# Order of the second FFN in a one-core macaron block: up products issued one block ahead of down products

## The chip, the core and the metric

The kernel runs on one core of one Trainium2 chip. The metric is the device time of one execution, in microseconds. The kernel before was timed three times: median 276.64 us, from 276.61 to 277.13. Its profiled execution took 276.34 us, of which 274.4 us are the span from the first to the last instruction in the trace.

## What is computed

The input is a residual `x` of 2048 tokens by 128 features, in float32. Three sublayers follow one another, the same FFN weights being used twice:

```
x = x + 0.5 * ffn(layernorm(x))     # first FFN
x = x + attention(layernorm(x))     # 16 heads of 8, strided and local keys
x = x + 0.5 * ffn(layernorm(x))     # second FFN
ffn(h) = butterfly_down(gelu(butterfly_up(h @ W_exp + b_exp) + up_bias)) @ W_con + b_con + down_bias
```

The hidden width of the FFN is 512. The butterflies are linear, so the kernel folds them into the two weight matrices at its start: `UPW` (128 by 512) and `DNW` (512 by 128, held as four 128 by 128 pieces). What is left of an FFN per block of tokens is an up product, a gelu and a down product.

## The kernel before

The 2048 tokens are cut into four blocks of 512 (`NB` = 4, `QB` = 512), each of four tiles of 128 (`TB` = 4). Blocks are numbered through: 0 to 3 are the blocks of the first FFN, 4 to 7 those of the second. Block 7 belongs to the tokens of the last attention block, 4 to those of the first. Every engine has its own instruction list, written out by hand, and engines meet only at semaphores; nothing is reordered by a planner.

One block of the second FFN takes these steps. VectorE normalizes its four tiles into `XN[b % 2]` (`normalize`, called by `ffn_ahead(b - 1)`, which first waits until the transposes of block b - 1 have been done). TensorE transposes them into PSUM bank 0 (`transpose_block`). ScalarE copies them into `XT` (`operand`), which waits until the up product of the block before has read `XT`. TensorE makes the up product (`ffn_up`), four chunks of 128 hidden units into banks 1 to 4, each written as two matmul instructions in the trace. ScalarE applies gelu, chunk by chunk (`gelu`), from those banks into the single buffer `GH`; before its first chunk it waits for the down product of the block before (`y_ps`). TensorE makes the down product (`ffn_down`): 4 tiles by 4 chunks, 32 matmul instructions in the trace, into bank 5 (the first two tiles of blocks 3 and 7 go to bank 0, `down_bank`); before it starts it waits for all four gelus (`g_ready`) and for VectorE's sum of the block before (`y_done`), which has to have read bank 5. VectorE adds the bias to the residual `X` (`add_bias`) and then the product (`ffn_sum`, in two halves for blocks 3 and 7). SyncE writes the finished block out.

In the last part of TensorE's list (lines 720 to 729) the order is: last value products of attention, transposes of block 4, `turn`, up product 4, `ctx_turn`, `project` (output projection of the last attention block, which waits for VectorE's copy `CTT`, line 1148); then for each block: its up product (block 4's is already there), the transposes of the next block, its down product. ScalarE's list there is gelu 4, operand 5, gelu 5, operand 6 and so on. VectorE's is: the last `finish_unit`, `finish_block(3)` (lines 1146 to 1151), the layernorm statistics of the last tokens, sum 4, then `ffn_ahead(5)` (which normalizes block 6), sum 5, `ffn_ahead(6)`, sum 6, sum 7. Block 5 has been normalized long before, within attention.

`ARENA` is a large SBUF tile; its first 8192 columns hold the attention probabilities (`PE_`).

Of the kernel before, what the change touches and what calls it, by code (L numbers as in the profile page):

```python
# [12 lines left out]
ACT = mybir.ActivationFunctionType  # L13
# [3 lines left out]
P = 128  # L17
S = 2048
NT = S // P
QB = 512  # L20
NB = S // QB
TB = QB // P
HID = 512
NC = HID // P
# [36 lines left out]
def program(nc, x, q_w, k_w, v_w, o_w, o_b, unity, w_exp_t, b_exp, up_near, up_far, up_b, dn_w, w_con, b_con, dn_b,  # L61
# [5 lines left out]
    with ctx:  # L67
        def sb(name, shape, dt=F32):
            return ctx.enter_context(nc.sbuf_tensor(name, shape, dt))

        def sem(name):
            return ctx.enter_context(nc.semaphore(name))
# [10 lines left out]
        GH = sb("gelu_h", [P, NC, QB])  # L83
# [6 lines left out]
        DNW = sb("down_folded", [P, NC, P])  # L90
        WCON = sb("w_con_sb", [P, NC, P])
        ARENA = sb("probs_all", [P, 10 * SC])
        BEX = sb("b_exp_sb", [P, NC])
        UBC = sb("up_bias_sb", [P, NC])
        BUP = sb("bias_up", [P, NC])
# [57 lines left out]
        PS = ctx.enter_context(nc.psum_tensor("ps", [P, 8, 512], F32))  # L153
# [35 lines left out]
        g_ready = sem("g_ready")  # L189
        y_ps = sem("y_ps")  # L190
        y_half = sem("y_half")
        y_first = sem("y_first")
        y_done = sem("y_done")
# [66 lines left out]
        def split_seen(b, part):  # L260
            return 4 * b + 4 if b < NB - 2 else 4 * (NB - 2) + 4 * last_splits.index((b, part)) + 4

        def down_bank(b, t):
            return PS[:, 0, :] if b % NB == NB - 1 and t < 2 else PS[:, 5, :]

# [161 lines left out]
        def _(pe):  # L427
# [9 lines left out]
            def ffn_up(b, chunks=range(NC)):  # L437

                pe.wait_ge(xt_ready, b + 1)
                if 2 <= b < NB:  # L440
                    pe.wait_ge(qk_ready, 3 * (b - 1))
                for c in chunks:
                    if 2 <= b < NB and c == 2:
                        pe.wait_ge(v_ready, 3 * (b - 1))
                    if b % NB:
                        pe.wait_ge(g_ready, NC * (b - 1) + c + 1)
                    pe.matmul(PS[:, 1 + c, :], UPW[:, c * P:(c + 1) * P], XT[:, :], start=True, stop=True).then_inc(h_ps, 1)  # L447
# [3 lines left out]
            for r in range(NC):  # L451
                mm = pe.matmul(PS[:, (6, 7, 4, 5)[r], :], ONE[32 * r:32 * r + 1, :], WUF[32 * r:32 * r + 1, :], start=True, stop=True)
# [5 lines left out]
            for j in range(NC):  # L458
                pe.wait_ge(wc_mix, j + 1)
                for o in range(NC):  # L460
                    mm = pe.matmul(PS[:, 2, j * P:(j + 1) * P], DNB[-1][:, j * P:(j + 1) * P], WCM[:, o, j, :],  # L461
                                   start=(o == 0), stop=(o == NC - 1))
# [4 lines left out]
            for j in range(NC):  # L467
                mm = pe.matmul(PS[:, 3, j:j + 1], UPB[STAGES - 3][:, j * P:(j + 1) * P], BEX[:, j:j + 1], start=True, stop=True)
            mm.then_inc(bup_ps, 1)
            pe.wait_ge(ld_wt, 16)  # L470
            for c in range(NC):
                pe.wait_ge(up_fold, STAGES - 2 + c + 1)
                mm = pe.matmul(PS[:, 1, :], WT[:, c, :], UPB[-1][:, c * HID:(c + 1) * HID], start=(c == 0), stop=(c == NC - 1))  # L473
# [6 lines left out]
            def ffn_down(b):  # L480
                if b == 0:
                    pe.wait_ge(dnw_sb, 1)
                pe.wait_ge(g_ready, NC * (b + 1))
                if b % NB:
                    pe.wait_ge(y_done, b)
                for t in range(TB):
                    for c in range(NC):
                        mm = pe.matmul(down_bank(b, t)[:, t * P:(t + 1) * P], GH[:, c, t * P:(t + 1) * P], DNW[:, c, :],  # L488
                                       start=(c == 0), stop=(c == NC - 1))
                    if t == 1 and b % NB == NB - 1:  # L490
                        mm.then_inc(y_half, 1)
                mm.then_inc(y_ps, 1)
# [92 lines left out]
            with nc.body("pe_large_bound", valid_engines=[pe.engine]):  # L585
                for b in range(NB):
                    pe.wait_ge(ld_ks[b], 16 * PARTS)
                for it in range(NB):
                    pe.wait_ge(ld_mq, 16 * (PARTS + 1) * NG * (it + 1))
                    for t in range(TB):  # L590
                        for j in range(NG + 1):
# [6 lines left out]
                            if j < NG:  # L598
                                for h in range(G):
                                    mm = pe.matmul(PS[:, half + h, :], QS[0:PROD, j, h, t * P:(t + 1) * P],  # L600
                                                   KS[0:PROD, :, G * j + h, :], start=True, stop=True)
                            else:
                                for c in range(2):
# [3 lines left out]
                                    for h in range(8):  # L607
                                        hh = 8 * c + h
                                        for w in range(2):
                                            q0 = t * P + w * W  # L610
                                            k0 = (2 * t + w) * WSTEP
                                            mm = pe.matmul(PS[w * W:(w + 1) * W, half + c, h * WIN:(h + 1) * WIN],
                                                           QS[0:PROD, hh // G, hh % G, q0:q0 + W],
                                                           KL[0:PROD, hh // G, hh % G, k0:k0 + WIN],
                                                           start=False, stop=(h == 7), skip_group_check=True)
# [67 lines left out]
            def ctx_turn(it):  # L683
                pe.wait_ge(o_ctx, 2 * NG * (it + 1))
                for t in range(TB):
                    mm = pe.transpose(PS[:, 7, t * P:(t + 1) * P], CT[:, t, :], ID[:, :])
                mm.then_inc(ct_ps, 1)

            def project(it):
                pe.wait_ge(ct_sb, it + 1)  # L690
                for t in range(TB):
                    mm = pe.matmul(PS[:, 7, t * P:(t + 1) * P], CTT[:, t * P:(t + 1) * P], OW[:, :], start=True, stop=True)  # L692
                mm.then_inc(op_ps, 1)
# [26 lines left out]
            turn(NB - 1, NG - 1)  # L720
            ffn_up(NB)
            ctx_turn(NB - 1)
            project(NB - 1)

            for b in range(NB, 2 * NB):
                if b > NB:
                    ffn_up(b)
                if b < 2 * NB - 1:
                    transpose_block(b + 1)
                ffn_down(b)  # L730

        @block.scalar
        def _(act):
# [15 lines left out]
            def gelu(b):  # L750
                for c in range(NC):
                    act.wait_ge(h_ps, NC * b + c + 1)
                    if b and c == 0:
                        act.wait_ge(y_ps, b)
                    if b == 0 and c == 0:
                        act.wait_ge(bup_set, 1)
                    act.activation(GH[:, c, :], PS[:, 1 + c, :], ACT.Gelu, bias=BUP[:, c:c + 1]).then_inc(g_ready, 1)  # L757

            def squares(b):
                act.wait_ge(qk_ready, 3 * b + 3)  # L760
# [116 lines left out]
        def _(dve):  # L877
# [37 lines left out]
            def layernorm(a, n):  # L915
                moments(a, n)
                rstd(a, n)
# [81 lines left out]
            def ffn_ahead(b):  # L999
                dve.wait_ge(xt_ps, b)  # L1000
                normalize(b + 1, XN, xn_ready)
# [6 lines left out]
            def ffn_sum(b):  # L1008
                add_bias(b)
                dve.wait_ge(r_ready, b + 2)  # L1010
                last = b % NB == NB - 1
                if last:
                    dve.wait_ge(y_half, b // NB + 1)
                    sum_tiles(b, 0, 2, y_first)
                    if b < NB:
                        dve.wait_ge(y_first, 1)
                        statistics(b * TB, 2)
                dve.wait_ge(y_ps, b + 1)
                sum_tiles(b, 2 if last else 0, TB, y_done)
# [107 lines left out]
            def finish_unit(it, g):  # L1127
                n = NG * it + g
                dve.wait_ge(o_ps, n + 1)
                if n:  # L1130
                    dve.wait_ge(ot_ps, n)
                dve.tensor_copy(OS[:, :], PS[:, 6 + n % 2, 0:QB // 2]).then_inc(o_sb, 1)  # L1132
                dve.wait_ge(ot_ps, n + 1)
                ov = PS[:, 6 + n % 2, QB // 2:QB].rearrange("p (t h c) -> p t h c", t=2, h=G)
                dve.reciprocal(RD[:, :, :, :], ov[:, :, :, D:D + V1 + 1:V1]).then_inc(o_den, 1)  # L1135
                dve.wait_ge(o_den, n + 1)
                if g == 0 and it:
                    dve.wait_ge(ct_ps, it)
                for r in range(2):
                    dve.tensor_tensor(CT[:, r:TB:2, G * D * g:G * D * (g + 1)].rearrange("p t (h d) -> p t h d", h=G),  # L1140
                                      ov[:, :, :, r * V1:r * V1 + D], RD[:, :, :, r:r + 1].to_broadcast([P, 2, G, D]),
                                      ALU.mult).then_inc(o_ctx, 1)

            def finish_block(it):
                ts = slice(it * TB, it * TB + TB)
                dve.tensor_tensor(X[:, ts, :], X[:, ts, :], OBB[:, None, :].to_broadcast([P, TB, P]), ALU.add).then_inc(obias_added, 1)
                dve.wait_ge(ct_ps, it + 1)
                dve.tensor_copy(CTT[:, :], PS[:, 7, :]).then_inc(ct_sb, 1)  # L1148
                dve.wait_ge(obias_added, it + 1)
                dve.wait_ge(op_ps, it + 1)  # L1150
                dve.tensor_tensor(X[:, ts, :], PS[:, 7, :].rearrange("p (t d) -> p t d", t=TB), X[:, ts, :],
                                  ALU.add).then_inc(x2_done, 1)
# [10 lines left out]
            for it in range(NB):  # L1163
                for g in range(NG):
# [13 lines left out]
                    if it == 2 and g == 2:  # L1178
                        ffn_ahead(NB)
            finish_unit(NB - 1, NG - 1)  # L1180
            finish_block(NB - 1)
            dve.wait_ge(x2_done, NB)
            layernorm((NB - 1) * TB, TB)
            ffn_sum(NB)
            for b in range(NB + 1, 2 * NB):
                if b < 2 * NB - 1:
                    ffn_ahead(b)
                ffn_sum(b)

# [95 lines left out]
```

## Time and profile before

| | |
|---|---|
| median of 3 runs | 276.64 us (276.61 to 277.13) |
| profiled execution | 276.34 us |
| its span | 274.4 us |
| outside the span | 1.9 us |
| TensorE busy | 251.5 us, 92% of the span |
| ScalarE busy | 197.1 us, 72% |
| VectorE busy | 126.6 us, 46% |
| granted TensorE clock, mean | 0.999 |

The second FFN is what is left after attention: from about 236 us to the end. The names in a row say which engine worked, on which line of the kernel, what it wrote and read, and how often; a bracket tells how long the engine had been idle before and what released it. "PE" is TensorE's matmul, "PEld" its weight load, "DVE" VectorE, "ACT" ScalarE, "SPq" SyncE's queue.

### The profile page before, as it was taken

Reading aid. Unit: us, or ns where it says so; the run is one execution under the profiler, and the core shown is the slowest. Engines: PE = TensorE matmul, PEld = TensorE weight load, DVE = VectorE, ACT = ScalarE, POOL = GpSimd, SP = SyncE. Lnnn points to the kernel's source line nnn. Section 1 sums busy time; section 2 is a strip of 40 time slices with the busy share of each in tenths; the row PEclk is TensorE's granted clock in tenths of the full one; section 3 lists DMA queues with packets and bytes.
Section 4 is the critical chain, followed back from the end, with each engine's and each line's share of the span. In section 5 each row is a group of like instructions: output and inputs, shape, how many; then the busy total and the mean of one; then the engine's idle time right before and its main releaser. Section 6 shows DMA issues by size and latency. Waiting matters only on the chain.

```text
span 274.4 us, 6943 instructions
## 1 busy us (share of the span) xinstructions
PE 251.5 (92%) x2921; PEld 137.6 (50%) x2921; DVE 126.6 (46%) x408; ACT 197.1 (72%) x256; POOL 7.3 (3%) x12
## 2 busy tenths in 40 slices
PE   2697899999889999899999899999899999889995
PEld 0473675866434444345444354444454444476665
DVE  4986549897693033225234225324324520554311
ACT  0854347586759999887999887999878999624430
POOL 9100000000000000000000000000000000000000
PEclk9999999999999999999999999999999999999999
DMA  6940000486679541230331231233030000001111
GB/s 212 249 118 7 2 1 0 157 213 180 164 234 334 186 94 26 78 84 2 86 84 42 41 84 30 57 84 75 9 84 2 4 0 2 2 0 41 38 38 38
DMA packets 23887, 21.82 MB, mean 80 GB/s; under 512 B 4743, under 2 KB 22087, under 8 KB 23835
## 3 DMA queue, kind: packets, MB, share of 16 engines
q1 hardware_dynamic: 22742, 21.02, 28.4%
q8 instruction: 24, 0.39, 0.6%
q10 hardware_dynamic: 1112, 0.34, 0.6%
q14 instruction: 9, 0.07, 0.1%
HBM read 13.98 MB, written 7.56 MB: 79 GB/s over the span
## 4 chain that ended last, share of the span: by engine, by line
PE 84%; ACT 8%; DVE 5%; issue 1%; DMA 1%; DVEq 0%; ACTq 0%
PE ps L662 22%; PE ps L640 21%; PE ps L488 11%; PE ps L447 9%; PE ps L672 3%; PE ps L647 3%; PE ps L461 2%; PE ps L692 2%; ACT probs_all L863 2%; PE ps L680 1%; PE ps L473 1%; ACT gelu_h L757 1%; PE ps L523 1%; DMA resid<-L_attn_x 1%; DVE ctx_t L1148 1%
## 5 line engine op out<-in xcount | busy, mean ns | idle before, releaser
L859 ACT ACTIVATE probs_all<-ps 128x1024 f32<-128x1024 f32 x128 | 123.0, 1023 | 15.9 <-PE ps L640 12.3
L662 PE MATMUL ps<-probs_all,v_strided 128*32 128x256 f32 x1024 | 68.2, 384 | 0.2 <-ACT probs_all L859 0.2
L640 PE MATMUL ps<-q_slots,k_strided 75*128 75x512 bf16 x250 | 64.7, 381 | 2.9 <-ACT probs_all L863 2.5
L662 PEld LDWEIGHTS ps<-probs_all,v_strided 128*32 128x32 f32 x1024 | 27.1, 109 | 31.9 <-issue 10.8
L640 PEld LDWEIGHTS ps<-q_slots,k_strided 75*128 75x128 bf16 x250 | 20.4, 97 | 37.4 <-issue 11.7
L1135 DVE RECIPROCAL rden<-ps 128x16 f32<-128x16 f32 x16 | 4.1, 257 | 72.2 <-PE ps L680 72.2
L757 ACT ACTIVATE gelu_h<-ps,bias_up 128x512 f32<-128x512 f32 x32 | 21.8, 687 | 19.8 <-PE ps L447 19.7
L488 PE MATMUL ps<-down_folded,gelu_h 128*128 128x128 f32 x256 | 30.5, 277 | 2.7 <-ACT gelu_h L757 2.7
L488 PEld LDWEIGHTS ps<-down_folded,gelu_h 128*128 128x128 f32 x256 | 29.2, 192 | 5.2 <-ACT gelu_h L757 3.3
L447 PE MATMUL ps<-xnorm_t,up_folded 128*128 128x512 f32 x64 | 29.3, 600 | 1.7 <-ACT xnorm_t L748 1.0
L1161 DVE SCALAR_TENSOR_TENSOR probs_all<-probs_all,mask_k_sb 128x1024 f32<-128x1024 f32 x16 | 19.6, 1223 | 4.5 <-ACT probs_all L863 4.0
L863 ACT ACTIVATE probs_all<-ps 128x1024 f32<-128x1024 f32 x16 | 16.4, 1023 | 3.6 <-PE ps L647 2.1
L447 PEld LDWEIGHTS ps<-xnorm_t,up_folded 128*128 128x128 f32 x64 | 11.5, 190 | 14.8 <-issue 10.9
L1005 DVE SCALAR_TENSOR_TENSOR resid<-ps,resid 128x512 f32<-128x512 f32 (+1 forms) x10 | 5.9, 585 | 27.5 <-PE ps L488 27.4
L1132 DVE COPY o_sb<-ps 128x256 f32<-128x256 f32 x16 | 6.8, 424 | 16.5 <-PE ps L672 15.2
L647 PEld LDWEIGHTS ps<-q_slots,k_local 75*64 75x64 bf16 x512 | 9.3, 112 | 5.9 <-ACT probs_all L859 5.4
L924 DVE TENSOR_SCALAR xnorm<-resid,mean_var,rstd 128x128 f32<-128x128 f32 x44 | 12.1, 341 | 0.2
L672 PEld LDWEIGHTS ps<-probs_all,v_local 128*32 128x32 f32 x512 | 7.9, 109 | 7.9 <-issue 5.9
L890 DVE BATCH_NORM_STATS2 stats<-resid 128x6 f32<-128x128 f32 x48 | 10.3, 280 | 2.8 <-DMA resid<-L_attn_x 2.6
L672 PE MATMUL ps<-probs_all,v_local 128*32 128x64 f32 x512 | 10.5, 222 | 1.0 <-DVE probs_all L1161 1.0
L647 PE MATMUL ps<-q_slots,k_local 75*64 75x64 bf16 x512 | 11.1, 197 | 0.0
L748 ACT ACTIVATE xnorm_t<-ps 128x512 f32<-128x512 f32 x8 | 4.7, 593 | 8.6 <-PE ps L434 8.6
(116 smaller groups left out, 207.7 us busy)
## 6 DMA issues: line engine op xcount, KB each, us to landing
q_slots<-q_parts SPq DMA_DIRECT2D x16, 288.0 KB
k_local<-k_local_parts SPq DMA_DIRECT2D x48, 78.0 KB
q_parts<-prologue_or_parts SPq DMA_DIRECT2D x9, 384.0 KB, 4.0
k_strided<-k_strided_parts SPq DMA_DIRECT2D x12, 96.0 KB
q_parts<-last_parts SPq DMA_DIRECT2D x3, 384.0 KB, 5.1
k_local_parts<-prologue_or_parts SPq DMA_DIRECT2D x3, 288.0 KB, 5.1
resid<-L_attn_x SPq DMA_DIRECT2D x1, 768.0 KB, 10.2
out<-resid SPq DMA_DIRECT2D x3, 256.0 KB, 2.3
```

What stands on the lines that cost most here:

```text
L447: pe.matmul(PS[:, 1 + c, :], UPW[:, c * P:(c + 1) * P], XT[:, :], start=True, stop=True).then_inc(h_ps, 1)
L488: mm = pe.matmul(down_bank(b, t)[:, t * P:(t + 1) * P], GH[:, c, t * P:(t + 1) * P], DNW[:, c, :], start=(c == 0), stop=(c == NC - 1))
L640: mm = pe.matmul(PS[:, b0 + i, :], KS[:, ch, G * g + h, :], QS[:, g, h, :], start=True, stop=True)
L647: mm = pe.matmul(PS[r * W:(r + 1) * W, b0 + h // 2, (h % 2 * TB + t) * W:(h % 2 * TB + t + 1) * W], KL[:, g, h, w * WSTEP:w * WSTEP + W], ...
L662: mm = pe.matmul(PS[VC * h:VC * (h + 1), 6 + n % 2, 0:QB // 2], VS[:, ch, at:at + VC], probs, start=(ch == 0 and r == 0), stop=False, skip ...
L672: mm = pe.matmul(PS[VC * h:VC * (h + 1), 6 + n % 2, t * W:(t + 1) * W], VL[:, TB * it + t, at:at + VC], PL[:, h, t, :], start=False, stop= ...
L757: act.activation(GH[:, c, :], PS[:, 1 + c, :], ACT.Gelu, bias=BUP[:, c:c + 1]).then_inc(g_ready, 1)
L859: act.activation(PE_[:, ch // 2, 2 * m:2 * m + 2, ch % 2, :], PS[:, b0:b0 + 2, :], ACT.Exp).then_inc(p_ready, 1)
L863: act.activation(PL[:, :, :, :].rearrange("p h t q -> p (h t q)"), PS[:, b0:b0 + 2, :].rearrange("p a b -> p (a b)"), ACT.Exp).then_inc(p_ ...
L890: ln_link(dve.bn_stats(STAT[:, t, :], X[:, t, :]))
L924: dve.tensor_scalar(xn[:, t, :], X[:, i, :], MV[:, i, 0:1], RS[:, i:i + 1], ALU.subtract, ALU.mult).then_inc(done, 1)
L1161: dve.scalar_tensor_tensor(pl, pl, 3.0e38, band, ALU.min, ALU.mult).then_inc(pl_ready, 1)
```

## The change

The second FFN is reordered so that a block's up product stands ahead of the down product of the block before it. Four places follow from that. (1) The gelu results alternate between two buffers: even blocks in `GH`, blocks 5 and 7 in the first 2048 columns of `ARENA`; gelu 6 and 7 wait only for the down product two blocks back. (2) TensorE's list: the transposes of block 5 stand ahead of `project(3)`; then come up 5, transposes 6, down 4, up 6, transposes 7, down 5, up 7, down 6, down 7. (3) VectorE's list: `ffn_ahead(5)` stands ahead of `finish_block(3)`, `ffn_ahead(6)` ahead of sum 4. (4) In the down products of blocks 3 and 7 the wait for the sum of the block before stands at the third tile, which is the first that goes to bank 5.

```diff
+        def hidden(b):
+            return GH if b % 2 == 0 or b < NB else ARENA[:, 0:NC * QB].rearrange("p (c q) -> p c q", c=NC)
+
...
                 pe.wait_ge(g_ready, NC * (b + 1))
-                if b % NB:
+                last = b % NB == NB - 1
+                if b % NB and not last:
                     pe.wait_ge(y_done, b)
                 for t in range(TB):
+                    if last and t == 2:
+                        pe.wait_ge(y_done, b)
                     for c in range(NC):
-                        mm = pe.matmul(down_bank(b, t)[:, t * P:(t + 1) * P], GH[:, c, t * P:(t + 1) * P], DNW[:, c, :],
+                        mm = pe.matmul(down_bank(b, t)[:, t * P:(t + 1) * P], hidden(b)[:, c, t * P:(t + 1) * P], DNW[:, c, :],
                                        start=(c == 0), stop=(c == NC - 1))
...
             turn(NB - 1, NG - 1)
             ffn_up(NB)
             ctx_turn(NB - 1)
+
+            transpose_block(NB + 1)
             project(NB - 1)
-
-            for b in range(NB, 2 * NB):
-                if b > NB:
-                    ffn_up(b)
+            for b in range(NB + 1, 2 * NB):
+                ffn_up(b)
                 if b < 2 * NB - 1:
                     transpose_block(b + 1)
-                ffn_down(b)
+                ffn_down(b - 1)
+            ffn_down(2 * NB - 1)
...
                     if b and c == 0:
-                        act.wait_ge(y_ps, b)
+                        act.wait_ge(y_ps, b if b <= NB else b - 1)
                     if b == 0 and c == 0:
                         act.wait_ge(bup_set, 1)
-                    act.activation(GH[:, c, :], PS[:, 1 + c, :], ACT.Gelu, bias=BUP[:, c:c + 1]).then_inc(g_ready, 1)
+                    act.activation(hidden(b)[:, c, :], PS[:, 1 + c, :], ACT.Gelu, bias=BUP[:, c:c + 1]).then_inc(g_ready, 1)
...
             finish_unit(NB - 1, NG - 1)
+            ffn_ahead(NB + 1)
             finish_block(NB - 1)
             dve.wait_ge(x2_done, NB)
             layernorm((NB - 1) * TB, TB)
-            ffn_sum(NB)
-            for b in range(NB + 1, 2 * NB):
-                if b < 2 * NB - 1:
-                    ffn_ahead(b)
+            ffn_ahead(NB + 2)
+            for b in range(NB, 2 * NB):
                 ffn_sum(b)
```

## Rows read from the trace of the kernel before

**Rows 1.** The profile's page: the chain that ended last, shares by engine and line.

```profile
PE 84%; ACT 8%; DVE 5%; issue 1%; DMA 1%; DVEq 0%; ACTq 0%
```

**Rows 2.** The chain from 241 us, in order: start us, length us, what.

```profile
241.58 0.70 DVE ctx_t L1148
...
242.32 1.16 PE ps L692 x8
243.48 0.44 PE ps L434 x4
243.91 3.57 PE ps L488 x32
247.49 3.45 PE ps L447 x8
...
250.96 0.70 ACT gelu_h L757
...
251.70 3.84 PE ps L488 x32
255.54 3.45 PE ps L447 x8
...
267.81 3.85 PE ps L488 x32
...
271.68 0.42 DVE resid L1005
```

**Rows 3.** TensorE and ScalarE, order of time: start us, length us, what [idle before].

```profile
241.14 0.69 ACT L757 ACTIVATE gelu_h<-ps,bias_up 128x512 f32<-128x512 f32 x1 [0.17 <-PE ps L447]
...
243.75 3.74 PE L488 MATMUL ps<-down_folded,gelu_h 128*128 128x128 f32 x32
243.95 0.60 ACT L748 ACTIVATE xnorm_t<-ps 128x512 f32<-128x512 f32 x1 [2.13 <-PE ps L434]
...
247.32 3.60 PE L447 MATMUL ps<-xnorm_t,up_folded 128*128 128x512 f32 x8
...
250.76 0.60 PE L434 MATMUL ps<-ident_sb,xnorm 128*128 128x128 f32 x4
...
255.38 3.60 PE L447 MATMUL ps<-xnorm_t,up_folded 128*128 128x512 f32 x8
...
263.43 3.60 PE L447 MATMUL ps<-xnorm_t,up_folded 128*128 128x512 f32 x8
```

**Rows 4.** VectorE's instructions in the same view.

```profile
237.45 0.36 DVE L1140 TENSOR_TENSOR ctx_rows<-ps,rden 128x64 f32<-128x64 f32 x2
237.72 0.68 DVE L1146 TENSOR_TENSOR resid<-resid,o_bias 128x512 f32<-128x512 f32 x1
...
248.75 1.10 DVE L924 TENSOR_SCALAR xnorm<-resid,mean_var,rstd 128x128 f32<-128x128 f32 x4
...
263.70 0.69 DVE L1005 SCALAR_TENSOR_TENSOR resid<-ps,resid 128x512 f32<-128x512 f32 x1 [5.74 <-PE ps L488]
264.31 0.68 DVE L931 SCALAR_TENSOR_TENSOR resid<-ffn_bias,resid 128x512 f32<-128x512 f32 x1
```

**Rows 5.** SyncE's queue in order of time: the last two writes of the output.

```profile
270.42 0.37 SPq L405 DMA_DIRECT2D out<-resid  x1
272.13 0.37 SPq L407 DMA_DIRECT2D out<-resid  x1
```

**Rows 6.** DMA issues of the page: count, KB each, median us to landing.

```profile
out<-resid SPq DMA_DIRECT2D x3, 256.0 KB, 2.3
...
out<-resid SPq DMA_DIRECT2D x2, 128.0 KB, 1.8
```

**Rows 7.** Stretches: busy us and count of each engine, then PEclk, DMA share, GB/s.

```profile
60.00:235.00 175.00, 168.83 (x2441) 80.91 (x2441) 69.51 (x202) 151.53 (x170) 0.00 (x0) 1.00 0.31 83
...
271.60:274.40 2.80, 0.04 (x1) 0.00 (x0) 0.42 (x1) 0.00 (x0) 0.00 (x0) 0.93 0.23 66
```

**Rows 8.** TensorE in order of time, at down product 3 of the first FFN.

```profile
59.95 3.84 PE L488 MATMUL ps<-down_folded,gelu_h 128*128 128x128 f32 x32 [0.34 <-ACT gelu_h L757]
```

## Prediction

> **What bounds the kernel now.** I read the chain of work that ended last first, because only what stands on it can shorten the run. It is 84% TensorE [rows 1]; the shares of busy time say the same for the whole kernel but not for the stretch that is changed, so I then read the chain from 241 us on, piece by piece [rows 2]. There TensorE is handed over only three times to another engine: after each of up products 5, 6 and 7 the chain goes through a gelu (0.70 us) before the down product of the same block starts. The first of these is shown: the up product ends at 247.49 + 3.45 = 250.94, the down product starts at 251.70. The pattern repeats with the same numbers for block 6 (8.05 us later), and block 7 has 0.78 in place of 0.76. VectorE's sums, ScalarE's operand copies and the output DMAs are not on the chain until the last sum at 271.68. So the tail is bound by TensorE's work plus three exposed gelus.
>
> **What the change removes.** In the new order each down product has another block's up product between it and its gelu, or a whole down product (block 7), so the gelu has 3.5 us or more of cover for its 0.7.
>
> (a) Three gelu waits: 0.76 + 0.76 + 0.78 = 2.30 us [rows 2].
>
> (b) A down product that starts after the wait takes 3.84, 3.84 and 3.85 us from the start of its first product to its end, and one that follows other work directly adds 3.57 (down 4, end to end) [rows 2]. The overlap with the end of the work before it comes back: 0.27 + 0.27 + 0.28 = 0.82 us.
>
> (c) The transposes of block 5 are 0.44 us on the chain between `project` and down 4 [rows 2]. Now they stand ahead of `project`, which in any case waits for the copy of `ctx_t` from 241.58 to 242.28. The context transposes end just before 241.58, four transposes end about 0.44 us later, at 242.0, before `project` can start at 242.32. Gain 0.44 us; if the cover were gone, 0.
>
> **What it costs.** (d) The transposes of blocks 6 and 7 ran under the gelu wait (the first at 250.76, while the gelu ran at 250.96) [rows 2, 3]. There is no wait left to hide them, so each adds the 0.44 us that four transposes take on the chain when nothing covers them [rows 2]: 0.88 us.
>
> Sum: 2.30 + 0.82 + 0.44 - 0.88 = 2.68 us less. A count by starts, which does not use modelled ends, checks it. One period, from up 5 at 247.32 to up 6 at 255.38, is 8.06 us [rows 3]. Without waits it is up to transposes 3.44 (247.32 to 250.76), transposes to down 0.44, down to up 3.57 (243.75 to 247.32), together 7.45 [rows 2, 3]. Two periods save 2 x 0.61 = 1.22. The last up and down product took 267.81 - 263.43 + 3.84 = 8.22 [rows 2, 3] and will take 3.44 + 3.74 = 7.18, which saves 1.04. With (c) that is 2.70. Both counts agree; I use 2.67, from the schedule below.
>
> **Schedule after**, by ends on TensorE, with 3.45 per up, 3.57 per down and 0.44 per set of transposes [rows 2]: `project` ends at 243.48 as before; up 5 246.93; transposes 6 247.37; down 4 250.94; up 6 254.39; transposes 7 254.83; down 5 258.40; up 7 261.85; down 6 265.42; down 7 268.99. Before, down 7 ended at 271.66 [rows 2]. Now every wait in it, with what stands behind the waiting instruction:
>
> - Up 5 needs `XT` of block 5. ScalarE is free at 241.83 [rows 3], transposes 5 end at 242.0, the copy takes 0.60 [rows 3]: 242.6, against 243.3, where the first product of up 5 can start (an up product starts 0.17 before the work ahead of it ends, 247.32 against 247.49). Slack 0.7 us. It is the tightest on TensorE; whatever it were late would push everything behind it.
> - The `XT` copies of blocks 6 and 7 follow the last gelu of blocks 5 and 6: ready at about 248.3 and 255.7, needed at 250.9 and 258.4. Slack 2.6 us.
> - Gelu 6 waits for down 4 (250.94) and its own first chunk (about 251.8); gelu 7 for down 5 (258.40) and its chunk (about 259.3). The new waits cost nothing, and ScalarE has nothing else queued but those copies. Gelu 7 ends at about 262.6, needed at 265.4.
> - `ffn_ahead(5)` is four normalizations, 1.10 us together [rows 4], now ahead of `finish_block(3)`: the context rows end at 237.81, then 1.10 and the bias addition of 0.68, so 239.6. The copy of `ctx_t`, on the chain, can't start before 241.58 anyway [rows 2]: VectorE idled from 238.40 to then, 3.18 us [rows 4]. Hidden; 2.0 us of slack.
> - `ffn_ahead(6)` comes before the bias and sum of block 4 where its twin `ffn_ahead(5)` came behind them, at 248.75 to 249.85 [rows 4]. It ends by 249.85 even so; transposes 7 need it at 254.4. What is queued behind it on VectorE is the bias of block 4 and sum 4, whose product is ready only at 250.94.
> - Down 5 needs sum 4 (251.66, slack 3 us), down 6 needs sum 5 (259.1, slack 2.7). Down 7 needs sum 6 (265.42 + 0.02 + 0.69 = 266.1) only at its third tile, at about 267.2: slack 1.1. If the wait stood at its start it would cost 0.7, so this split is what keeps the last gap shut.
> - Bias 7 (0.68) comes after sum 6 and ends at 266.8; the first half of sum 7 is due at 267.2. It was at 264.31 before [rows 4] and is now the tightest of VectorE, 0.4 us, but a late first half only delays a write that isn't the last.
> - In the first FFN down 3 had its wait for the sum moved too. It waited for the gelu [rows 8], and the rows of block 2 that TensorE had already transposed come from that sum, so the wait was already met. Zero.
>
> After down 7 the sum of two tiles and a write follow as before: 0.42, then issue at 272.13 and the end of the span at 274.4 [rows 2, 5]. The write of block 6 now is issued at about 266.2 instead of 264.4 and lands 2.3 us later [rows 6], at 268.5; the first two tiles go at about 267.7, the last at about 269.5. The last two stay 1.7 to 1.8 us apart as before [rows 5], so I take zero; if the write of block 6 and the two after it had to be served one behind the other, 266.2 + 2.3 + 1.8 + 1.8 = 272.1 against 271.7, at most 0.4 us.
>
> The waits added (one per down product 7 and 3) show nowhere in the trace; I take 0, bounded above by 0.04 each, the step from a semaphore to the next start between the gelu's end and the down product (251.66 to 251.70) [rows 2], and below by 0, since no work goes.
>
> **A rule weighed against the rows.** Term (b) rests on rows alone. The Trainium skill ("TensorE: Matmul & The Clock Gate", Single matmul latency) gives a lone product a constant of 398 cycles at 2.4 GHz on top of its columns, 166 ns, which a stream hides. By that, as an estimate, (b) would be 3 x 0.166 = 0.50 in place of 0.82 and the time 0.3 us longer; the rows, with 0.27 per start, decide for me.
>
> **The rivals.**
>
> R1, partial gain. The chain's ends are modelled, and something small keeps each start open: all of (b) stays. Then 2.68 - 0.82 = 1.86 less, 274.8 us. Against it: up 6 takes 3.45 directly behind down 5, and the count by starts gives the sum without using an end. 6%.
>
> R2, the chain moves to a copy. `XT` of block 5 comes later than `project` ends, because ScalarE works off gelu 4 first; or the transposes of block 5, now in front, delay `project`. The price is at most what (c) gained, 0.44, and a 0.60 copy in the open: 276.64 - 2.68 + 1.04 = 275.0. For it: only 0.7 us of slack. 4%.
>
> R3, it does not do what it says: the three waits come back as waits on something else (the sums, bank 5 being one buffer). That needs a step that is late by more than the 2.7 us of slack of down 6. 276.6 us. 2%.
>
> **How the numbers follow.** The profiled execution: 276.34 - 2.67 = 273.67 us, span 274.4 - 2.7 = 271.7. It lay 0.30 under the median of the runs, so the median is 276.64 - 2.67 = 273.97, say 274.0. This case has 85%. Its own bounds: down to 273.5 (the runs before spread by 0.5), up to 274.5 (the writes 0.4, two waits 0.08). To hold 8 in 10, and since R1 and R2 are near, I take 273.4 to 274.9. What can be told from no change is about 0.2%, 0.55 us. Faster by more: forecast, R1 and R2, 95%. Within: R3, 2%. Slower: R4, 3%.
>
> **What would show it.** In the changed profile no wait of line 488 for line 757 after 240 us; the chain from 243 us one row of TensorE, with transposes of line 434 in it twice; transposes 5 before the eight products of line 692; up 5 starting at about 243.3 instead of 247.3; down 7 ending near 269.0; the sum at 269.0. An idle entry on TensorE before up 5 would mean R2; down products of 3.8 us on the chain R1; waits of line 488 for line 1005 R3; a PEclk under 1 between 245 and 269 R4. I am wrong if TensorE's list from `project` on takes other than 25.5 us.

## The result, and the profile after

The changed kernel takes 274.62 us (median of 19 runs, 273.61 to 276.44) and the kernel before 277.02 us (19 runs beside them, 276.23 to 279.35). The ratio is 0.9913, with a 95% interval of 0.9886 to 0.9941: faster, clear of the 0.2% that can be told. The forecast was 274.0 in a range of 273.4 to 274.9. The profiled execution took 273.61 us with a span of 271.6; the sum made against the profiled execution had said 273.67 and 271.7.

Some executions of either kernel have a mean granted clock of 0.994 or less in place of 0.999 or more and take some 2.2 us more (last section), so the medians compared from here on are those of the executions without it, with their number beside them. In the comparison above that leaves 274.18 us (10 of 19) against 276.90 (13 of 19, for the kernel before told apart by their times): 2.72 us less. A repeat of the changed kernel on one chip gave 273.75 us (median of 4, 273.68 to 274.37) against 276.50 for the kernel before (19, 276.08 to 277.33): 2.75 us less.

The chain of work that ended last, of the changed kernel: start us, length us, what (with the line numbers of the changed file: L450 is the up product, L437 the transposes, L494 the down product, L698 the output projection, L1012 the sum).

```profile
241.48 0.70 DVE ctx_t L1155
...
242.22 1.16 PE ps L698 x8
243.38 3.44 PE ps L450 x8
246.82 0.44 PE ps L437 x4
247.25 3.57 PE ps L494 x32
250.83 3.44 PE ps L450 x8
254.26 0.44 PE ps L437 x4
254.70 3.57 PE ps L494 x32
258.27 3.44 PE ps L450 x8
261.71 7.16 PE ps L494 x64
268.87 0.02 issue
268.89 0.42 DVE resid L1012
```

Against [rows 2] the gelus are gone, from the projection to the last sum there is one engine, and the transposes appear twice. Down product 7 ends at 268.87, forecast at 268.99.

What the engines do beside it, in order of time, in the changed kernel:

```profile
237.62 1.11 DVE L931 TENSOR_SCALAR xnorm<-resid,mean_var,rstd 128x128 f32<-128x128 f32 x4
...
241.28 0.60 PE L437 MATMUL ps<-ident_sb,xnorm 128*128 128x128 f32 x4
241.48 0.69 DVE L1155 COPY ctx_t<-ps 128x512 f32<-128x512 f32 x1 [2.15 <-PE ps L692]
241.91 0.60 ACT L755 ACTIVATE xnorm_t<-ps 128x512 f32<-128x512 f32 x1 [0.19 <-PE ps L437]
242.22 1.16 PE L698 MATMUL ps<-o_w_sb,ctx_t 128*128 128x128 f32 x8 [0.35 <-DVE ctx_t L1155]
243.22 3.60 PE L450 MATMUL ps<-xnorm_t,up_folded 128*128 128x512 f32 x8
...
265.39 0.69 DVE L1012 SCALAR_TENSOR_TENSOR resid<-ps,resid 128x512 f32<-128x512 f32 x1 [5.72 <-PE ps L494]
266.00 0.68 DVE L938 SCALAR_TENSOR_TENSOR resid<-ffn_bias,resid 128x512 f32<-128x512 f32 x1
267.17 0.42 DVE L1012 SCALAR_TENSOR_TENSOR resid<-ps,resid 128x256 f32<-128x256 f32 x1 [0.50 <-PE ps L494]
```

The four transposes of block 5 stand in the wait for the context copy; the projection's idle time before it is 0.35 us. The operand copy ends at 242.51 and up product 5 starts at 243.22: the tightest slack, 0.7 us as worked out. Bias 7 ends at 266.68, and VectorE then waits 0.50 us for the first half of down 7 (forecast slack 0.4). The gapless stretch, as busy us and count of each engine, then the granted clock (PEclk), DMA share, GB/s:

```profile
243.00:269.00 26.00, 25.85 (x164) 19.82 (x162) 9.54 (x31) 9.22 (x14) 0.00 (x0) 1.00 0.12 36
```

TensorE was busy 25.85 of 26 us, at a PEclk of 1.00.

To compare profiles whose earlier parts differ by a few tenths, I take the length of the tail from the start of up product 4 to the start of the last sum, both in the chain. Before: 237.40 to 271.68, 34.28 us. After: 237.30 to 268.89, 31.59 us; in the repeat 237.58 to 269.16, 31.58. That is 2.69 us less. The repeat agrees to a hundredth, so the tail tells smaller differences than the times do, which differ by up to a microsecond between executions of one kernel.

### The profile page after: what moved, and what is told of

Its sections match the earlier page's. It is cut to its first block, busy times and chain, and to the rows that moved or that the text cites. A ratio compares the mean times of both kernels' runs of the same rounds, so it can differ in the third digit from the quotient of the medians.

```text
span 271.6 us, 6941 instructions
## 1 busy us (share of the span) xinstructions
PE 250.6 (92%) x2921; PEld 137.5 (51%) x2921; DVE 126.6 (47%) x408; ACT 197.2 (73%) x256; POOL 7.3 (3%) x12
## 4 chain that ended last, share of the span: by engine, by line
PE 85%; ACT 7%; DVE 5%; issue 1%; DMA 1%; DVEq 0%; ACTq 0%
PE ps L668 22%; PE ps L646 22%; PE ps L494 11%; PE ps L450 9%; PE ps L678 3%; PE ps L653 3%; PE ps L464 2%; PE ps L698 2%; ACT probs_all L870 2%; PE ps L686 1%; PE ps L476 1%; PE ps L437 1%; PE ps L529 1%; DMA resid<-L_attn_x 1%; DVE ctx_t L1155 1%
## 5 line engine op out<-in xcount | busy, mean ns | idle before, releaser
L450 PE MATMUL ps<-xnorm_t,up_folded 128*128 128x512 f32 x64 | 29.3, 600 | 1.7 <-ACT xnorm_t L755 1.0
L494 PE MATMUL ps<-down_folded,gelu_h 128*128 128x128 f32 x192 | 22.7, 276 | 1.2 <-ACT gelu_h L764 1.2
L764 ACT ACTIVATE gelu_h<-ps,bias_up 128x512 f32<-128x512 f32 x24 | 16.4, 687 | 10.0 <-PE ps L450 9.9
L494 PEld LDWEIGHTS ps<-down_folded,gelu_h 128*128 128x128 f32 x192 | 22.0, 192 | 2.9 <-issue 2.1
L450 PEld LDWEIGHTS ps<-xnorm_t,up_folded 128*128 128x128 f32 x64 | 11.5, 190 | 14.8 <-issue 10.9
L1012 DVE SCALAR_TENSOR_TENSOR resid<-ps,resid 128x512 f32<-128x512 f32 (+1 forms) x10 | 5.8, 585 | 25.8 <-PE ps L494 25.8
L764 ACT ACTIVATE probs_all<-ps,bias_up 128x512 f32<-128x512 f32 x8 | 5.5, 687 | 6.5 <-PE ps L450 6.5
```

Of the source, the lines that this page charges most:

```text
L494: mm = pe.matmul(down_bank(b, t)[:, t * P:(t + 1) * P], hidden(b)[:, c, t * P:(t + 1) * P], DNW[:, c, :], start=(c == 0), stop=(c == NC - 1))
L764: act.activation(hidden(b)[:, c, :], PS[:, 1 + c, :], ACT.Gelu, bias=BUP[:, c:c + 1]).then_inc(g_ready, 1)
```

## The experiments

A time given without a median is that of a single execution.

**The changed kernel again.** 

> The changed kernel as it is, again, for a tight interval beside the kernel before and as the base of the next three. Theory (three exposed gelus and their restarts gone, transposes 5 hidden, transposes 6 and 7 now in the open): 2.7 us less than the kernel before, ratio 0.990. Rival R4 (lower granted clock in the gapless stretch): a PEclk under 1 between 243 and 269 us and less than 2 us of gain.

273.75 us (median of 4 of 6), 2.75 less than the kernel before; ratio over all runs 0.9894 (0.9844 to 0.9944). Tail 31.58 us. R4 has no sign.

**The gelu doubled, in the kernel before and in the changed one.** This asks directly whether the gelu is covered.

```
                     if b == 0 and c == 0:
                         act.wait_ge(bup_set, 1)
+                    if b > NB:
+                        act.activation(ARENA[:, (4 * (b - NB) + c) * QB:(4 * (b - NB) + c + 1) * QB], PS[:, 1 + c, :], ACT.Gelu, bias=BUP[:, c:c + 1])
                     act.activation(...)
```

> The kernel before, with a second gelu of the same size (its result goes to unused columns) ahead of each gelu of blocks 5, 6 and 7. Theory (the gelu is exposed after each up product): ScalarE needs 8 x 0.69 from its first chunk instead of ending 4.3 us after the up product's start, 2.25 us later per block, 6.8 us slower than the kernel before. If gelus were hidden there (rival): 0.

Measured 284.4 us against 276.76 in a run beside it, 7.6 more; the tail is 237.65 to 279.59, 41.94 us, 7.66 more. The waits of the down product (us in total, times, longest), and then TensorE's rows in order of time:

```profile
PE ps L488 <- ACT gelu_h L759: 5.9, 3, 2.2
```

```profile
253.42 3.84 PE L488 MATMUL ps<-down_folded,gelu_h 128*128 128x128 f32 x32 [1.81 <-ACT gelu_h L759]
...
262.94 5.46 PE L488 MATMUL ps<-down_folded,gelu_h 128*128 128x128 f32 x32 [1.81 <-ACT gelu_h L759]
...
274.09 5.46 PE L488 MATMUL ps<-down_folded,gelu_h 128*128 128x128 f32 x32 [2.25 <-ACT gelu_h L759]
```

The wait rose from 1.5 us in three to 5.9 us in three: 4.4 us, not the 6.8 expected. Doubled gelus followed each other at 0.58 us, though each row reads 0.69; with 0.58 the last gelu ends 1.5 us later per block, 4.4 in three. The other 3.2 us are two down products of 5.46 in place of 3.84, at the lower clock (0.66 in the stretch from 263 to 268 us). The theory (exposed) stands, with a wrong price per gelu; that the time came out near the expected one, 7.6 against 6.8, is luck, since the clock made up for what the gelus cost less.

> The same doubling in the changed kernel. Theory (another product covers the gelu): the operand copy behind the doubled gelus ends at about 250.4 and 257.8, needed at 250.66 and 258.1; gelu 7 ends at 264.7, needed at 265.1: 0 to 0.3 us slower than the changed kernel. If the gelu were still on the path: 6.8 us.

Measured 273.91 us; tail 237.48 to 269.06, 31.58 us, the same as without the doubling. From 240 us on TensorE has one wait:

```profile
PE ps L698 <- DVE ctx_t L1157: 0.3, 1, 0.3
```

The same work on ScalarE that costs the kernel before 7.7 us (4.4 of it wait, the rest clock) costs the changed one nothing.

**Transposes of block 5 behind the projection**, in the changed kernel.

```
-            transpose_block(NB + 1)
             project(NB - 1)
+            transpose_block(NB + 1)
```

> The changed kernel with the transposes of block 5 back behind the output projection. By term (c) of the prediction this costs 0.44 us. By the rows of the changed kernel it costs more, since in the new order up 5 comes directly behind and needs the copy of those transposes: they would end at 243.8, the copy 0.60 later, so up 5 would start at 244.5 instead of 243.2, which is 1.3 us slower than the changed kernel.

Measured 275.28 us (median of 9, against 273.75 and 276.50 on the same chip), 1.5 more than the changed kernel; tail 237.51 to 270.49, 32.98 us, 1.40 more. The chain:

```profile
242.43 1.16 PE ps L698 x8
243.59 0.45 PE ps L437 x4
244.04 0.02 issue
244.06 0.61 ACT xnorm_t L755
244.67 0.04 issue
244.71 3.70 PE ps L450 x8
```

The move is worth 1.4 us in the new order: 0.44 for the transposes, 0.67 for the copy and its two semaphore steps, and 0.26 for the restart of the up product (3.70 in place of 3.44). In the old order down 4 lay over that copy.

**The same move alone in the kernel before**: `transpose_block(NB + 1)` ahead of `project(NB - 1)`, and left out of the loop.

> One part of the change alone, in the kernel before: the transposes of block 5 stand ahead of the output projection, nothing else is changed. Term (c) of the prediction: 0.44 us less than the kernel before. Rival (they delay the projection, or the gain is lost in the wait for the first gelu): 0 or slower.

Tail 240.19 to 274.04, 33.85 us, 0.43 less than before, as term (c) says. The timed runs don't show it: 276.56 us (median of 8) against 276.61 (7 of the kernel before), where single executions spread over more than 1 us; over all runs the ratio is 0.9961 (0.9923 to 0.9999). The chain shows the 0.43, the total leaves it open.

**One transpose in place of four, blocks 6 and 7**, in the changed kernel. It leaves out three quarters of those transposes, so three of four tiles of their operand are not computed.

```
-                for t in range(TB):
+                for t in range(TB) if b <= NB + 1 else (TB - 1,):
```

> The changed kernel with one transpose in place of four for each of blocks 6 and 7, so three quarters of these transposes are left out (the operand of those blocks is then wrong in three tiles). Term (d): they are in the open now, 0.11 us each, so six fewer save 0.66 us of the chain between up 5 and the end. If they were hidden: 0.

Measured 273.15 us; tail 237.46 to 268.39, 30.93 us, 0.66 less than after. The rows of the chain read 0.11 where they read 0.44. Term (d) is right.

**Two more copies ahead of the operand copy of block 5**, in the changed kernel.

```
             def operand(b):
...
+                if b == NB + 1:
+                    for r in range(2):
+                        act.activation(ARENA[:, (4 + r) * QB:(5 + r) * QB], PS[:, 0, :], ACT.Copy)
                 act.activation(XT[:, :], PS[:, 0, :], ACT.Copy).then_inc(xt_ready, 1)
```

> The changed kernel with two more copies of the same size (to unused columns) ahead of the operand copy of block 5, the step with the least slack. Theory: the slack is 0.7 us (copy ends at 242.51, up 5 starts at 243.22), two copies of 0.60 ahead use it up and cost 0.5 us. If the copy were on the path already (R2): 1.2 us.

Tail 239.67 to 271.68, 32.01 us, 0.42 more than after. (The whole execution took 276.48 us, with a granted clock of 0.72 from 70 to 76 us.) In order of time:

```profile
244.28 1.08 ACT L757 ACTIVATE probs_all<-ps 128x512 f32<-128x512 f32 x2 [0.18 <-PE ps L437]
...
245.25 0.60 ACT L758 ACTIVATE xnorm_t<-ps 128x512 f32<-128x512 f32 x1
...
245.91 3.70 PE L450 MATMUL ps<-xnorm_t,up_folded 128*128 128x512 f32 x8 [0.16 <-ACT xnorm_t L758]
```

The projection starts at 244.59 there, and up 5 comes 1.32 us behind it instead of 1.00. So of 0.97 us of added copies (244.28 to 245.25) 0.65 were covered: the slack worked out as 0.7 us is there, and R2 was not the case.

**The wait for the sum at the start of down products 3 and 7**, in the changed kernel.

```
-                if b % NB and not last:
+                if b % NB:
                     pe.wait_ge(y_done, b)
                 for t in range(TB):
-                    if last and t == 2:
-                        pe.wait_ge(y_done, b)
```

> The changed kernel with the wait of down products 3 and 7 for the sum of the block before put back to their start. The prediction gave that wait 0.7 us. By the rows of the changed kernel, sum 6 ends at 266.08 and down 7 started at 265.12, so with 0.04 for the semaphore it is 1.0 us slower than the changed kernel. If the sum were hidden anyway (rival): 0. In the first FFN: 0 by both.

Measured 275.23 us (median of 6), 1.5 more than the changed kernel; tail 238.08 to 270.85, 32.77 us, 1.19 more. The chain:

```profile
262.49 3.59 PE ps L492 x32
...
266.17 0.70 DVE resid L1010
266.87 0.14 issue
267.00 3.82 PE ps L492 x32
```

TensorE stands still from 266.07 to 267.00, 0.93 us, and pays the restart (3.82 in place of 3.57). Both earlier prices, 0.7 and 1.0, left out the restart. The other 0.3 us of the timed difference are not in the tail, and down 3 of the first FFN waits 0.34 us for its gelu with the edit and without it, so the edit costs nothing there. What differs is the kernel's first long product, 6.02 us in this profile and 5.52 in that of the repeat, which the edit does not touch and which varies from execution to execution (last section).

**One buffer for the gelu results**, in the changed kernel: `hidden(b)` is `GH` for all blocks, and the gelu waits for `y_ps` of the block before.

```
-            return GH if b % 2 == 0 or b < NB else ARENA[:, 0:NC * QB].rearrange("p (c q) -> p c q", c=NC)
+            return GH
...
-                        act.wait_ge(y_ps, b if b <= NB else b - 1)
+                        act.wait_ge(y_ps, b)
```

> The changed kernel with one buffer for the gelu results: all blocks write to the one tile, and each gelu waits for the down product of the block before. The order of the products stays. Theory: gelu 5 starts only at 250.85, so the copy behind it ends 3.6 us late for up 6; the same again for up 7; and gelu 7 waits for down 6, so down 7 starts 3 us late: 10 us slower than the changed kernel, 7.6 us slower than the kernel before. Rival (the order alone brings the gain): no more than 1 us.

Measured 288.52 us, against 276.76 for the kernel before in a run beside it; tail 237.86 to 283.81, 45.95 us, 14.4 more than after. Waits from 240 us on (us in total, times, longest):

```profile
PE ps L450 <- ACT xnorm_t L755: 6.1, 2, 3.1
PE ps L494 <- ACT gelu_h L764: 2.6, 1, 2.6
```

One stretch behind such a wait, as busy us and count of each engine, then PEclk:

```profile
254.00:260.00 6.00, 5.56 (x12) 2.60 (x13) 0.00 (x0) 0.39 (x1) 0.00 (x0) 0.72 0.03 6
```

The waits are where they were expected, 8.7 us instead of some 10, since gelus in a row are quicker than single ones. What was not expected is the clock behind them: after 3.06 us without work TensorE goes on at a PEclk of 0.72. Up products 6 and 7 take 5.34 and 5.40 us in the chain in place of 3.44, the last down product 5.40 in place of 3.58. That is 5.7 us, of which some 0.8 would be the three restarts at the price seen elsewhere (0.26 each), and with 8.7 it makes the 14.4. The order without the second buffer is a loss. The buffer without the order was not run; in the kernel before it had nothing to shorten, since each first gelu there is released by its up product and not by the down product before it (gelu 5 starts at 248.39, 0.90 us after down 4 ended at 247.49). So order and buffer pay only together.

**Down product 4 ahead of the projection**, in the changed kernel, to fill the rest of the wait.

```
             transpose_block(NB + 1)
+            ffn_down(NB)
             project(NB - 1)
...
-                ffn_down(b - 1)
+                if b > NB + 1:
+                    ffn_down(b - 1)
```

> The changed kernel with down product 4 moved ahead of the output projection, so that it fills the rest of the wait for the copy of the context (TensorE idle from 241.9 to 242.2) and the projection follows other work directly. Theory: 0.3 us of idle time and about 0.3 us of restart go, 0.6 us faster than the changed kernel. Rival: the projection comes 3.6 us later, so layernorm of the last tokens ends 3.6 us later (about 251), the normalization of block 7 at about 252; if that were late for its transposes at 254.3 the gain turns into a wait on line 931.

Measured 274.90 us (median of 9), 1.15 more than the changed kernel; tail 239.93 to 272.17, 32.24 us, 0.65 more. Not the 0.6 gain, and not by the rival: the wait is at up 6, for an operand copy.

```profile
253.20 0.59 ACT L757 ACTIVATE xnorm_t<-ps 128x512 f32<-128x512 f32 x1
253.84 1.55 PE L450 MATMUL ps<-xnorm_t,up_folded 128*128 128x512 f32 x3 [0.83 <-ACT xnorm_t L757]
```

Down 4 had been the longest piece between up 5 and up 6. Without it only transposes cover the last gelu of block 5 and the copy behind it: in the chain up 6 starts 1.25 us after up 5 ended (252.59 to 253.84).

**Half of down product 4 ahead of the projection**, in the changed kernel: tiles 0 and 1 there, tiles 2 and 3 behind transposes 6.

```
-            def ffn_down(b):
+            def ffn_down(b, tiles=range(TB)):
...
             transpose_block(NB + 1)
+            ffn_down(NB, range(2))
             project(NB - 1)
...
-                ffn_down(b - 1)
+                ffn_down(b - 1, range(2 if b == NB + 1 else 0, TB))
```

> The changed kernel with only the first two tiles of down product 4 moved ahead of the output projection, the other two left behind transposes 6. In the run where all of down 4 was moved, up 6 waited 1.25 us for the last gelu of block 5 and the copy behind it, since only transposes 6 stood between up 5 and up 6. Theory: half a down product (1.8 us) and the transposes (0.44) cover those 1.25 us, and the projection's wait is filled: the 0.3 us of idle time and 0.3 us of restart go, 0.6 us faster than the changed kernel, about 273.4 us where the changed kernel takes 274.0. If the later projection is what costs (rival), a wait on line 931 or 1012 appears and it is slower.

Measured 273.34 us (median of 4, 272.97 to 273.96) against 276.61 for the kernel before beside it (7): 3.3 us less; ratio over all runs 0.9876 (0.982 to 0.9931). Tail 237.88 to 269.02, 31.14 us, 0.45 less than after. The chain:

```profile
242.01 0.44 PE ps L437 x4
242.45 1.96 PE ps L494 x16
244.41 0.89 PE ps L699 x8
245.30 3.44 PE ps L450 x8
248.73 0.44 PE ps L437 x4
249.17 1.79 PE ps L494 x16
250.96 3.44 PE ps L450 x8
```

From up 4 on TensorE has no wait that the chain shows. Expected were 0.6: the first half takes 1.96 in place of the 1.79 of the second, probably because its gelu (241.61 to 242.30) ends only just as it begins. By the tail this order beats both kernels. It was not timed beside the changed kernel: 273.34 and 273.75 us come from two comparisons, whose kernels before took 276.61 and 276.50.

## Why the prediction was right

- (a) and (b), the waits and restarts, 2.30 and 0.82: right. No wait of the down product is left after 240 us, two down products in a row take 7.16 us in the chain, 3.58 each, and the doubled gelu (7.7 us in the old order, 0 in the new) shows that it is cover and not a shorter gelu.
- The rule weighed against (b): the Trainium skill ("TensorE: Matmul & The Clock Gate", Single matmul latency) would have made (b) 0.50, as an estimate. The trace disagrees for these float32 products: by the page 2.36 us would have gone in all, 2.69 went, and where an experiment put a new wait ahead of a product at the full clock, the product paid 0.25 or 0.26 on top (3.82 for 3.57, 3.70 for 3.44).
- (c), transposes of block 5: 0.43 measured alone in the old order, 0.44 forecast. Within the new order it is worth 1.4, since there the operand copy would be bare too. The sum was not touched by this, but the sentence "if the cover were gone, 0" undersold the move: it is a condition of the new order, not an extra. R2's price had the same gap: it put the transposes and the copy in the open at 1.04 us, and the run with just that lost 1.40, because the two semaphore steps (0.06) and the restart (0.26) came on top.
- (d), the transposes in the open, 0.88: right, 0.11 us for each.
- The schedule: slack of 0.7 us at up 5 confirmed by row and by the added copies; `ffn_ahead(5)` lay in VectorE's idle time at 237.62 to 238.73 and the context copy was not late; bias 7 had 0.5 us. The new place of the normalizations was not tried by itself: the old one can't be kept, since sum 4 waits for down 4, which stands behind transposes 6 in TensorE's list, and these wait for `ffn_ahead(5)`.
- The wait at the third tile of down 7: right that it is needed, mis-sized. The step said 0.7 if it stood at the start; the tail grew by 1.19 us. The term had the sum's length alone, without its semaphore steps and the restart. The slack of 1.1 us given for the third tile was too wide too: down 7 starts at 265.12, so by an estimate from its 3.57 us the third tile starts at about 266.9, 0.8 us after sum 6 ended (266.08).
- The writes: the last one is issued 0.45 us after the last sum starts, as before, and the span ends about 2.7 us behind that sum in both kernels (274.4 - 271.68, 271.6 - 268.89). Zero was right.
- R1, R2, R3: no row for them. R4: PEclk 1.00 through 26 us with 25.85 busy. Nine of the 19 executions of the changed kernel did have a lower mean clock, and none of these was profiled; but in the two variants of the changed kernel that were profiled with it (down 4 ahead, added copies) it fell at 72 us and read 1.00 from 243 to 269 us. In the tail the lower clock was seen only in kernels with longer waits there, the opposite of what R4 feared.
- The size: like against like it is 2.72 us by the times and 2.69 by the tail, against 2.67 forecast. That the median of all 19, 274.62, lay in the range is luck: it is the slowest of the ten executions at the full clock, and with one more at the lower it would have been 275.7 or so, outside the range. The prediction stood on three executions of the kernel before that by their times all had the full clock, and had no term for the others. The profiled execution came within 0.06 us of its own forecast, but it was the fastest of the 19; the tail is the better witness.

## What to carry to other kernels

When a chain alternates between TensorE and an activation of its result, issue the next block's first product ahead of this block's second, and count three things: the wait, the restart that it costs each time, and the small work that used to hide in the wait and now doesn't. Then list for each operand copy which product lies over it: moving a product to fill one gap can take away the cover of another, as the whole of down 4 did and half of it did not. Such an order needs a buffer more wherever the activation would overwrite what the delayed product still reads. And where whole executions vary by as much as the change is worth, compare one stretch of the trace: here it repeated to 0.01 us while the times spread over 1 us.

## What the runs showed of the hardware

The same kernel, at the same place, got the lower clock in one execution and not in the next. In the three profiles with a mean clock of 0.994 (down 4 ahead, added copies, and transposes moved in the kernel before) the clock fell at about 72 us, in a part of the program that none of them changed. TensorE around it, for the kernel before with the transposes of block 5 moved, in order of time:

```profile
69.48 0.39 PE L534 MATMUL ps<-squares,head_sel_sb 128*32 128x512 bf16 x2 [0.59 <-ACT squares L764]
...
71.52 0.67 PE L510 MATMUL ps<-xnorm_t,k_w_sb 128*128 128x128 f32 x2 [1.07 <-ACT xnorm_t L777]
72.02 1.81 PE L511 MATMUL ps<-xnorm_t,q_w_sb 128*128 128x512 f32 x2
```

The stretch in the same execution (busy us and count by engine, then PEclk):

```profile
72.00:74.00 2.00, 2.00 (x4) 0.91 (x3) 1.04 (x5) 0.91 (x4) 0.00 (x0) 0.54 0.85 163
```

A PEclk of 0.54 over 2 us is nearly all of it at 1.2 GHz. Before it TensorE was idle for 0.59 and 1.07 us within 2.7 us. But the kernel before's profile has the same two gaps and no fall, and its products of line 511 take 1.04 us in place of 1.81; so the gaps by themselves don't decide it. The stretch from line 510 to the product of `norms_max` takes 5.72 us with the fall (71.52 to 77.24) and 4.29 without (70.13 to 74.42): the fall costs 1.4 us, not the 2.2 that the times differ by.

The rest lies in the first long product of the kernel, here in the changed kernel's profile and in the one with the fall:

```profile
11.40 5.24 PE L464 MATMUL ps<-probs_all 128*128 128x128 f32 x32 [0.78 <-ACT probs_all L826]
```

```profile
11.39 6.74 PE L461 MATMUL ps<-probs_all 128*128 128x128 f32 x32 [0.79 <-ACT probs_all L820]
```

Later in the kernel 32 products of this size take 3.84 us behind a wait. Here they took 5.24 to 6.02 us in the ten profiles without a fall at 72 us and 6.30, 6.50 and 6.74 in the three with it, and PEclk reads 1.00 from 11 to 18 us in all thirteen, so that row doesn't show what slows them. From the end of this product to the start of up product 4 every profile without the fall takes 220.64 to 220.67 us: between these ten profiles the part ahead of the tail varies by this one product. That it also makes the spread of the other times was not traced. A long first product and a fall at 72 us went together; what makes either so long in some executions is open.

How often the lower mean clock was seen: in 9 of 19 executions of the changed kernel and, beside them, in 6 of 19 of the kernel before (by their times); later, on one chip, in 2 of 6 of the changed kernel and in 10 of 29 and 10 of 17 of the kernel before. The times differ by 2.0 to 2.2 us (276.20 against 274.18 after, 278.74 against 276.50 before). No kernel that closes the two gaps was tried.

In the tail, too, equal gaps had unequal ends. In the kernel before with doubled gelus the clock fell behind the second of two gaps of 1.81 us and not behind the first (5.46 and 3.84 us for the same down product), and with one gelu buffer it fell behind 3.06 us.

The second surprise is small: gelus or copies in a row on ScalarE follow each other at about 0.58 and 0.49 us, where the row of one reads 0.69 and 0.60. A cost taken from a lone row is about a fifth too high for a run of them.
